# Attention scores in three stretches a step, and a bias added by ScalarE, in a two-layer transformer kernel

## What is computed

```python
    x = _layernorm(x + _L0_attn_ref(x, ...), axis=-1)   # softmax(q k^T / sqrt(8)) v, 16 heads
    x = _layernorm(x + _L0_ffn_ref(x, ...), axis=-1)    # gelu(butterfly(x W_exp + b_exp) + up_bias) ...
    x = _layernorm(x + _L1_attn_ref(x, ...), axis=-1)   # the same with a causal mask and rope
    x = _layernorm(x + _L1_ffn_ref(x, ...), axis=-1)    # (silu(gate) * up) w_down
```

## Time and profile before

| | |
|---|---|
| median of 3 runs | 332.77 us (331.02 to 333.44) |
| the profiled execution | 331.46 us |
| its span in the profile | 329.7 us (1.8 us of the time lie around it) |
| mean granted TensorE clock | 0.955 |
| busy: TensorE, VectorE, ScalarE, GpSimd | 85%, 80%, 63%, 62% of the span |

### The profile page before, as it was taken

One profiled execution on the slowest core, in us unless ns is written; L12 is line 12 of the kernel. 1 busy time (PEld: TensorE's weight loads), 2 busy tenths in 40 slices (PEclk: granted clock), 3 DMA queues, 4 the chain that ended last, 5 costly groups with the idle time before them and its releaser, 6 DMA issues.

```text
span 329.7 us, 9464 instructions
## 1 busy us (share of the span) xinstructions
PE 281.9 (85%) x3194; PEld 199.3 (60%) x3194; DVE 263.6 (80%) x1007; ACT 207.4 (63%) x428; POOL 205.6 (62%) x326
## 2 busy tenths in 40 slices
PE   7989989997989989888997887988898888898763
PEld 3667555654666446554675456766676666666553
DVE  4897887879588888899679697687899999965565
ACT  2576865776857668496986569666385757536110
POOL 0549994471348447583779785697769756457332
PEclk9999969999899999999999799997799999899978
DMA  6684250303030220404022130403114040000000
GB/s 229 251 248 158 81 195 3 129 0 129 3 112 18 61 101 18 145 8 139 18 64 99 33 130 6 136 23 99 65 27 153 1 146 4 19 2 17 18 16 32
DMA packets 20495, 25.84 MB, mean 78 GB/s; under 512 B 3744, under 2 KB 14304, under 8 KB 20320
## 3 DMA queue, kind: packets, MB, share of 16 engines
q1 hardware_dynamic: 20016, 24.72, 22.4%
q10 hardware_dynamic: 432, 0.53, 0.5%
HBM read 6.36 MB, written 1.05 MB: 22 GB/s over the span
## 4 chain that ended last, share of the span: by engine, by line
PE 42%; DVE 32%; issue 12%; ACT 7%; POOL 4%; DMA 1%; POOLq 0%; ACTq 0%; DVEq 0%
PE bank L600 13%; DVE mx L824 7%; DVE room_c L832 6%; PE bank L615 4%; PE bank L398 4%; PE bank L388 4%; ACT E L728 3%; PE bank L465 3%; DVE turned L923 2%; PE bank L482 2%; DVE room_a L893 2%; DVE room_c L858 2%; PE bank L556 2%; PE bank L567 2%; DVE mx L832 2%
## 5 line engine op out<-in xcount | busy, mean ns | idle before, releaser
L728 ACT ACTIVATE E<-bank 128x512 f32<-128x512 f32 (+1 forms) x256 | 120.3, 550 | 78.4 <-PE bank L411 41.5
L824 DVE TENSOR_REDUCE mx<-bank 128x2 f32<-128x512 f32 x128 | 78.9, 679 | 9.3 <-PE bank L388 9.2
L832 DVE CUSTOM_DVE_ANT_0 room_c<-bank,mask_sb 128x256 f32<-128x256 f32 (+1 forms) x256 | 72.7, 349 | 1.3 <-PE bank L388 1.1
L398 PE MATMUL bank<-QK 32*128 32x256 f32 x480 | 55.8, 316 | 18.5 <-DVE hid L860 6.8
L388 PE MATMUL bank<-QK 32*128 32x256 f32 x480 | 56.8, 313 | 8.1 <-DVE mx L832 2.6
L600 PE MATMUL bank<-E,V 128*32 128x256 f32 (+1 forms) x1024 | 60.7, 383 | 0.1
L398 PEld LDWEIGHTS bank<-QK 32*128 32x128 f32 x480 | 36.9, 188 | 29.3 <-issue 21.8
L388 PEld LDWEIGHTS bank<-QK 32*128 32x128 f32 x480 | 37.2, 187 | 23.3 <-issue 8.9
L1052 POOL TENSOR_SCALAR_AFFINE_SELECT E<-E 128x512 f32<-128x512 f32 x64 | 39.2, 638 | 11.4 <-ACT E L728 11.3
L600 PEld LDWEIGHTS bank<-E,V 128*32 128x32 f32 x1024 | 31.5, 117 | 23.5 <-issue 7.0
L923 DVE STREAM_TRANSPOSE turned<-bank 128x256 f32<-128x256 f32 x32 | 14.3, 446 | 21.8 <-PE bank L600 21.8
(11 more groups left out here) (127 smaller groups left out, 558.7 us busy)
## 6 DMA issues: line engine op xcount, KB each, us to landing
spread_qk<-parts SPq DMA_DIRECT2D x30, 256.0 KB, 2.5
spread_qk<-parts SPq DMA_DIRECT2D x60, 128.0 KB, 2.1
room_c<-room_c SPq DMA_DIRECT2D x64, 32.0 KB, 1.9
xb<-x_nat SPq DMA_DIRECT2D x1, 1024.0 KB, 6.9
out<-ln_g SPq DMA_DIRECT2D x7, 128.0 KB, 1.9
xt<-x_t SPq DMA_DIRECT2D x1, 768.0 KB, 6.7
wi<-wi_all SPq DMA_DIRECT2D x1, 576.0 KB, 4.4
room_c<-fac_u SPq DMA_DIRECT2D x1, 508.0 KB, 6.5
```

The costliest lines, as they stand in the source:

```text
L398: nc.tensor.matmul(g_bank["exp", m][:, c * T:(c + 1) * T - q0], both[:, 1, c * P:(c + 1) * P], both[:, 0, q0:T], start=(c == 0), stop=False)
L728: act.activation(E[:, a % E_RING, j, 0:n], g_bank["exp", m][:, 0:n], ACT.Exp, scale=SCALE)\
L824: ins = nc.vector.tensor_reduce(mx[:, n % 2, :, i], bank[:, :].rearrange("p (q k) -> p q k", q=QT), AX.X, ALU.max, negate=True)
L832: ins = nc.vector.tensor_tensor_reduce(out=masked_s[:, at % 2, lo:hi], in0=bank[:, lo:hi], in1=mask_sb[:, T + lo - hi:T], scale=-1.0, scal ...
```

## The change

On TensorE the two parts of a step become three stretches (`step_scores`). The first has the maxima scores of g+14, g+15 and the exponential scores of g, g+1 in the same banks as before, but no `less_maximum`. The second has the exponential scores of g+2, g+3, and between them the `less_maximum` products of g and g+1. The third has the maxima scores of g+12, g+13, and between them the `less_maximum` products of g+2 and g+3. Waits for banks are placed at the head of a stretch: those for the banks of g+2 and g+3 ahead of the second, those for the maxima banks at+4, at+5 ahead of the third. The wait for `mt` stands ahead of the second instead of the first. Matmuls, their number, their banks and the order in which heads are done stay.

The copies of layer 0's way up go from VectorE (a tensor_scalar add) to ScalarE (an activation with the function Identity and `bias=bhid`), in the same steps, behind `xt` and ahead of `th`, the values and the high parts.

```diff
--- before.py
+++ after.py
@@ -412,12 +412,10 @@
                                                start=False, stop=(c == 1))
                 ins.then_inc(A["st_ps"], 1)
 
-            def scores(maxima, exps, at):
-
-                for i, m in enumerate(maxima):
-                    take((at + i) % BANKS, ("max", m), A["max_done"], order_of(m))
-                for i, m in enumerate(exps):
-                    take((at + len(maxima) + i) % BANKS, ("exp", m), A["exp_done"], m + 1)
+            def banks_for_maxima(maxima, i):
+                for m in maxima:
+                    take(i % BANKS, ("max", m), A["max_done"], order_of(m))
+                    i += 1
                 for m in maxima:
                     b, r, j = place(m)
                     if b == 0 and m % QUAD == 2:
@@ -426,19 +424,54 @@
                             pe.wait_ge(first_keys, 1)
                     elif b and m % 8 == 2:
                         pe.wait_ge(A["qk_ready"], 2 * (b - 1) + m % H // 8 + 1)
+
+            def banks_for_exps(exps, i):
                 for m in exps:
-                    if m % 8 == 0:
-                        pe.wait_ge(A["mt_ready"], m // 8 + 1)
-
-                first = exps and exps[0] % QUAD == 2
+                    take(i % BANKS, ("exp", m), A["exp_done"], m + 1)
+                    i += 1
+
+            def maxima_at_first(maxima, at):
+
+                banks_for_maxima(maxima, at)
+                for c in (1, 0):
+                    for m in maxima:
+                        max_scores(m, c)
+
+            def step_scores(g, at):
+
+
+                ahead = range(g + LEAD, g + LEAD + QUAD)
+                banks_for_maxima(ahead[2:], at)
+                banks_for_exps((g, g + 1), at + 2)
                 for long in range(2):
-                    for m in exps if first else ():
+                    for m in ahead[2:]:
+                        max_scores(m, 1 - long)
+                    for m in (g, g + 1):
                         exp_scores(m, long)
-                    for m in maxima:
-                        max_scores(m, 1 - long)
-                    for m in () if first else exps:
+                banks_for_exps((g + 2, g + 3), at + QUAD + 2)
+                if g % 8 == 0:
+                    pe.wait_ge(A["mt_ready"], g // 8 + 1)
+                for i in range(2):
+                    less_maximum(g + i)
+                    exp_scores(g + 2 + i, 0)
+                for i in range(2):
+                    exp_scores(g + 2 + i, 1)
+                banks_for_maxima(ahead[:2], at + QUAD)
+                for i in range(2):
+                    less_maximum(g + 2 + i)
+                    max_scores(ahead[i], 1)
+                for i in range(2):
+                    max_scores(ahead[i], 0)
+
+            def last_scores(g):
+
+                banks_for_exps(range(g, g + QUAD), 0)
+                if g % 8 == 0:
+                    pe.wait_ge(A["mt_ready"], g // 8 + 1)
+                for long in range(2):
+                    for m in range(g, g + QUAD):
                         exp_scores(m, long)
-                for m in exps:
+                for m in range(g, g + QUAD):
                     less_maximum(m)
 
             def project_group(r, i):
@@ -498,26 +531,25 @@
 
             project_group(0, 4)
             project(1, take(6, ("qk", 1), A["qk_out"], 2))
-            scores((2, 3), (), 0)
-            scores((0, 1), (), 2)
+            maxima_at_first((2, 3), 0)
+            maxima_at_first((0, 1), 2)
...
             for g in STEPS:
                 at = QUAD * (g // QUAD % 2)
                 claimed[0] = 0 if g <= HEADS else claimed[0]
                 if g + LEAD < HEADS:
-                    scores((g + LEAD + 2, g + LEAD + 3), (g, g + 1), at)
-                    scores((g + LEAD, g + LEAD + 1), (g + 2, g + 3), at + QUAD)
+                    step_scores(g, at)
                 elif g < HEADS:
-                    scores((), range(g, g + QUAD), 0)
+                    last_scores(g)
 
                 if (n := half_at(g, AT_MT)):
                     turn_maxima(n, claim(("mt", n), A["mt_ready"], n + 1, g))
@@ -744,6 +776,14 @@
                 if (n := tile_at(g, AT_XT0)) is not None:
                     act.wait_ge(F0["xt_ps"], n + 1)
                     act.activation(xt[:, n * FT:(n + 1) * FT], g_bank["xt0", n][:, :], ACT.Copy).then_inc(F0["xt_ready"], 1)
+                for c in range(HC):
+                    if (n := tile_at(g, AT_UP0[c])) is not None:
+                        if n == 0 and c == 0:
+                            act.wait_ge(bhid_ready, 1)
+                        if n and c == 0:
+                            act.wait_ge(F0["down_ps"], 2 * n)
+                        act.wait_ge(F0["up_ps"], HC * n + c + 1)
+                        act.activation(hid0[:, c, :], g_bank["up0", n, c][:, :], ACT.Identity, bias=bhid[:, c:c + 1]).then_inc(F0["pre_ready"], 1)
                 for b, c in ups_at(g):
                     i = SC * (b - NB) + c
                     act.wait_ge(F1["up_ps"], i + 1)
@@ -883,15 +923,6 @@
                     dve.wait_ge(F1["res_done"], b - NB - LN_RING + 1)
                     normalise_last(NA, b % LN_RING, A["ln_ready"])
 
-                for c in range(HC):
-                    if (n := tile_at(g, AT_UP0[c])) is not None:
-                        if n == 0 and c == 0:
-                            dve.wait_ge(bhid_ready, 1)
-                        if n and c == 0:
-                            dve.wait_ge(F0["down_ps"], 2 * n)
-                        dve.wait_ge(F0["up_ps"], HC * n + c + 1)
-                        nc.vector.tensor_scalar(hid0[:, c, :], g_bank["up0", n, c][:, :], bhid[:, c:c + 1], None, ALU.add)\
-                            .then_inc(F0["pre_ready"], 1)
                 for b, c in ups_at(g):
                     if (b, c) not in LATE_GATES:
                         gate(b, c)
```

More of the change, by code:

```diff
@@ L500, in _ @@
             project(1, take(6, ("qk", 1), A["qk_out"], 2))
-            scores((2, 3), (), 0)
-            scores((0, 1), (), 2)
+            maxima_at_first((2, 3), 0)
+            maxima_at_first((0, 1), 2)
             project_group(1, 7)
             project_group(2, 0)
-            scores((6, 7), (), 4)
-            scores((4, 5), (), 6)
+            maxima_at_first((6, 7), 4)
+            maxima_at_first((4, 5), 6)
             project_group(3, 1)
             project_values(0, take(3, ("v", 0), A["v_ready"], 1))
-            scores((10, 11), (), 4)
-            scores((8, 9), (), 6)
+            maxima_at_first((10, 11), 4)
+            maxima_at_first((8, 9), 6)
             turn_maxima(0, take(2, ("mt", 0), A["mt_ready"], 1))
```

## The result

The changed kernel takes 339.3 us by the median of four runs (337.14 to 340.68), the kernel before 331.89 us (327.56 to 333.44). The ratio is 1.0298, 95% interval [1.0152, 1.0444] (by the medians 1.022): slower by 2 to 3%, and outside the range that was given (up to 336.9 us). The profiled execution took 340.55 us, 9.1 more than the one of before.

A forecast was written before the change was run, and what follows sets the result against it. VectorE was taken to bound layer 1, and hand-overs between TensorE, VectorE and ScalarE through eight PSUM banks each step. Terms 2.8 + 0.7 - 1.0 - 2.3 - 1.1 + 0.5 = -0.4 us gave 332.4 us, range 328.2 to 336.9.

The forecast's parts named there:

- The sign of the whole: Whole kernel: gains of the tiles about equal to the losses of the wait, -0.4 us in sum; chance 0.38.
- the clock's term: A TensorE stretch near 1.2 GHz costs up to 1.6 us; one more or fewer inside the range, no chance of its own.
- Term (b): Layer 1: first two heads' exponentials start behind the wait for `hid`, VectorE's transpose moves 0.43 us; +2.8 us, bounds 0 and +7.
- Term (a): TensorE's scores in three stretches: taken as saving 0, bounds 0 and -3 us.
- Term (c): Layer 0: ScalarE's exponentials start up to 0.4 us later in about ten steps, partly covered by VectorE's maxima; +0.7 us.
- The four tiles: Layer 0's copies with bias before GELU, moved from VectorE to ScalarE: -3.9 us in sum.
- The first tile: Layer 0, 68 to 93 us: looser ScalarE, earlier table load, down projection gains more; -2.3 us, bounds -0.9 and -2.6.
- The third tile: Layer 0: a 1.06 us cast of QK on ScalarE ahead of the copies delays the scores; +0.5 us, bounds -1.0 and +1.3.
- The copy on ScalarE: Sixteen 128x512 copies with bias in layer 0: 597 ns each on ScalarE against 744 ns on VectorE.
- The rival "slower": Middle stretch's wait costs wherever a bank is late, in layer 0 too: +4.1 us, 336.9 us; chance 0.22.

The follow-up runs named there:

- the refilled kernel before: Four discarded 32x256 score matmuls a head put ahead of the first two exponential heads' scores in nine layer 1 steps, against the kernel before: 328.28 us, ratio 0.9965.

## Why the prediction was wrong, point by point

**The sign of the whole was lost on one sentence.** Under the rivals the prediction said of the clock that "one more or fewer is inside the range and has no chance of its own". The price it read was right (up to 1.6 us a stretch; a fall costs 1.2 to 1.6 us a pair here). What failed was the step to "one more or fewer", which put the clock's term in the sum at nothing. The change takes four matmuls from ahead of a wait that comes back in every pair of steps, so it doesn't add one fall, it adds a fall in most pairs: in the profiled execution one in each of the four pairs from step 204 to 236, at 1.5 us each, about 6 us. The earlier trace rows showed the place: TensorE idle for 1.08 us behind just these matmuls.

**Term (b), the lag in layer 1: mechanism right, size too small.** Forecast 0.43 us a pair, measured 0.56 at full clock (8.89 and 8.93 against 8.31 and 8.39). If all of the eight steps that it counted pay that, it is 4.5 us instead of 2.8; only the steady pairs from 204 on show it. The rows it named (L465, L578, L600, VectorE's transpose) moved in that order, each a little more than forecast: counted from the end of the wait, L465 came 0.40 us later instead of 0.34, L600 0.56 instead of 0.43. Where the last tenth comes from is open.

**Term (a), the stretches save nothing:** right. With early less-maximum matmuls in layer 1 and three stretches kept, nothing was gained over two parts (0.9945 against 0.9942).

**Term (c), the lag in layer 0, +0.7:** about right in size. Bias alone and bias with three stretches in layer 0 can be laid over each other: at step 96 the second is 0.60 us later (121.24 and 121.84 us), at step 116 0.95 (142.35 and 143.30).

**The four tiles, -3.9 us in sum:** right as a sum, wrong in two parts. The bias-only kernel was compared with the refilled kernel before (the same layer 0 as before) or with the kernel before itself, whichever has the upper clock there. Over the four steps to the first exponential behind each GELU it gains 0.82 (steps 48 to 64), 1.14 (80 to 96), 0.4 (112 to 128) and 1.14 us (148 to 160): 3.5 in sum, and 0.6 more lie in the steps between. The first tile was put at -2.3. The down projection of that term "had run late" because the matmuls ahead of it, L600 among them, ran at the lower clock:

```profile
83.12 2.79 PE L600 MATMUL bank<-E,V 128*32 128x256 f32 x32
```

This is the kernel before, whose profiled execution has the lower clock here; the refilled kernel before, with the same layer 0, has 1.00 in these microseconds, takes 1.93 us for the same 32 matmuls and is 0.7 us earlier behind this GELU. A fall of one execution was read as structure of the tile; that is about half of the 1.5 us by which the term was too large. The third tile was put at +0.5 and is -0.4 with the bias alone. In the changed kernel its step is a loss of 0.78 us (step 120), since both parts meet there. ScalarE and TensorE of the changed kernel:

```profile
148.10 1.30 ACT L786 ACTIVATE room_a<-bank,bhid 128x512 f32<-128x512 f32 x2
150.00 2.07 ACT L760 ACTIVATE E<-bank 128x512 f32<-128x512 f32 x4 [0.59 <-PE bank L407]
```

```profile
149.50 0.46 PE L407 MATMUL bank<-mt,const_r 32*128 32x512 f32 x1 [1.46 <-ACT room_a L786]
```

With the bias alone, the less-maximum matmuls are ahead of that wait, and ScalarE goes from the copies to the exponentials without a pause:

```profile
145.56 1.28 ACT L754 ACTIVATE room_a<-bank,bhid 128x512 f32<-128x512 f32 x2
146.70 2.10 ACT L728 ACTIVATE E<-bank 128x512 f32<-128x512 f32 x4
```

**The copy on ScalarE:** put at 597 ns from the one row of that size, measured 720:

```profile
L786 ACT ACTIVATE room_a<-bank,bhid x16: 689/720/756, 74.9 to 190.4; 128x512 f32<-128x512 f32 x16
```

It was hardly cheaper than VectorE's 744, so the part's gain is that the work moved to another engine, not that it shrank. It changed no term, as two copies behind one another overlap (1.28 to 1.30 us for two).

**The rival "slower"** named the right wait, and its condition was met: (b) over 0.5 us, measured 0.56. Its 336.9 us are by lag alone, without the clock's 6 us, so even the rival with the right sign was too low.

**What was to show it.** "No TENSOR_SCALAR of room_a on VectorE", "the first exponential of a step only after `hid`", and layer 0 ending 3 us earlier came as said. "A layer 1 batch 17.3 us instead of 16.7": it took 20.83 (252.88 to 273.71), and 17.82 with the clock up. (Two pairs at the forecast's own 0.4 us would have made 17.5.)

**The account,** from the two profiled executions: -3.15 to step 160, +5.21 from there to 204, +8.17 to 236, -1.13 to the end, together 9.1. In the third piece 4 x 0.56 = 2.2 are lag and 6 are clock. In the second the traces mix lag and clock (the changed kernel's was at 1.2 GHz from 223 to 233 us on end and once for three and a half, before's twice for three and a half); it was not split further.

## What to carry to other kernels

A wait of TensorE that comes back every step has two prices: the time, and the clock of what follows it. Before matmuls are moved from ahead of such a wait to behind it, read how long TensorE idles there and whether the clock holds, and allow for up to one fall per repetition, not one per kernel: in three profiled executions here it came in 20 of 27. A stretch at the lower clock in a single profile of before is not structure: compare with a second trace before a term rests on it.

## What the runs showed of the hardware

- TensorE's clock went from 2.4 to 1.2 GHz, mostly for some 3.5 us, in 20 of 27 pairs of steps when only score products stood ahead of a wait that left TensorE idle for 1.0 to 1.8 us (from step 204 on). With four more matmuls ahead of it and mostly 1.1 us idle it did so in 9 of 36. Matmuls on two of the four strips of 32 rows, with results that nobody reads, lowered both counts (to 6 of 18 and 3 of 27). The Trainium skill's page "TensorE: Matmul & The Clock Gate", in its section on psum-queue depth-cycling, says that short idle times between groups of matmuls made the clock of another kernel go up and down. This case's traces agree: 1.34 us idle at 262.89, and the lower clock behind it.
- One fall cost some 1.2 to 1.6 us in a pair that was otherwise bound by VectorE: 10.16 to 10.46 us against 8.90 in the changed kernel, and 9.59 against 8.39 in the pair from step 212 of the kernel with the stretches in layer 0 alone, where it came without the lag.
- An ACTIVATE of 128x512 from PSUM took 597 ns as a Copy and 720 ns as Identity with a bias per partition. The Trainium skill's page "ScalarE: Activation LUTs", in its section on what ACT_TABLE_LOAD costs, gives 186 ns and 0.833 ns an element, and 93 ns more for a bias of this kind, an estimate of 0.71 us. The trace agrees with 720 ns; the prediction had used the row of the plain copy.
- The profiled execution of the kernel with early less-maximum matmuls had a granted clock of 0.95 where the twelve others have 1.00, outside its falls, and was no slower for it (328.76 us):

```profile
100.00:140.00 40.00, 35.10 (x400) 23.99 (x402) 31.66 (x73) 30.96 (x60) 25.13 (x37) 0.95 0.21 67
```

Why is open.
